# Transformer block on one core: ScalarE scales two of three norms of the second stage, and its order of work changes

## The chip, the cores and the metric

The kernel runs on one core of a Trainium2 chip. The metric is the time of one execution in device microseconds, from the first to the last instruction with what the runtime adds around it. Less is better.

## What is computed

For X of 16 batches x 512 tokens x 256 features, in float32, four parts follow one another; `ln` is a layer norm without gain or bias.

```python
x = x + A(ln(x))      # 16 heads of 64, softmax, exact gelu, product with Wpost, plus its own input
x = x + F(ln(x))      # W1, W2 rounded to -1, 0, 1; relu between; 256 -> 1024 -> 256
x = x + B(ln(x))      # 16 heads of 16 with rotary positions and biases
x = x + F(ln(x))      # the same feed-forward part again
```

`ln` is (x - mean) / sqrt(var + 1e-5) over the 256 features of a token.

## The kernel before, in words

Everything is laid out by hand: SBUF is one arena in which tiles have fixed places, and some share one. Each of the five engines gets its own list of instructions, written by a loop over the same schedule; semaphores tie them together. The first stage is part A, in slots from -21 to 541 (LAST_A); the second stage is the rest of the block. The second stage counts in steps, two to a slot: step = 2 * (slot - SHIFT) with SHIFT = 554. A batch s has its steps at 64 * s + r, where r is the number in the tables of lines 296 to 305. Since the tables reach from r = -115 to 152, up to four batches are in work at a time: while the attention scores of batch s are made (r = 0 to 62), the feed-forward part in front of batch s + 1 or s + 2 and the one behind batch s - 1 or s - 2 fill the gaps. The two kinds are called ffn0 (before attention B) and ffn1 (after it); the norm in front of attention B is "attn".

Matrix products are split for precision: a value is held as a high part (rounded, type float32r) and a low part (the rest). A product's result lands in one of three PSUM banks taken in turn (`fill % 3`, line 229); a fill waits until the one three before it has been emptied.

The places that the change and the prediction touch:

- Norm, VectorE (lines 1070 to 1093): `statistics` of two token blocks in each of two pieces, `aggregate` (mean and variance of four blocks, then variance + eps into `rstd`), and `normalise` in two pieces of two blocks, each block one `tensor_scalar` (x - mean) * rstd into `xn`. The pieces 0 to 4 stand at the five steps of NORM. GpSimd raises `rstd` to the power -0.5 (lines 529 to 531), one step after piece 2. It adds the output bias to x after xn is made (`add_bias`, line 533, at BIAS).
- TensorE transposes `xn` (XT0, XTB, XT1; line 735); ScalarE copies the result to `xh` (line 852), VectorE makes `xl` (line 1164). The up products (UP0, UP1) start when both transposes' banks are emptied. ScalarE applies Relu (line 860) and makes the high part `h_hi` (line 880, `hidden_high`), GpSimd the low part `h_lo` (line 543); the down products (DOWN0, DOWN1) wait for the low parts in turn.
- Attention B: TensorE makes scores at every even step (line 691), VectorE takes row maxima (line 1114), which travel through a transposition (line 761) and a DMA on SP's queue into two rows of `q_stack`; L = 11 slots later TensorE makes the transposed scores (line 705), ScalarE takes their exponential (line 838) and TensorE the product with the values (line 718), four key blocks to a quad of heads. The sum of a quad is copied from PSUM by ScalarE (`copy_values`, line 847, at r = 40, 56, 72, 88), and the next quad's first product waits for it. VectorE turns it (`invert_sums`, at INVERT) and scales it (`scale_heads`).
- Rotary part: ScalarE empties the query and key products with their bias (line 865), GpSimd rotates (lines 552 and 556, at ROTATE; the keys of batch 0 are VectorE's), ScalarE writes high parts (`parts_high`, line 898, at HIGHS), VectorE low parts (`parts_low`, line 1110, at LOWS), and SP stacks both by DMA into `q_stack` and `k_stack` (at STACK). `h_hi` and `h_lo` lie over the buffers of the rotation, so the first `hidden_high` of a batch waits for `roped`.
- SP: `load_ahead` loads x of a batch into `x_ahead` at r = -115, after the batch before has been stored back; `save_ahead` stores it at r = -54, once the attention bias is added.

ScalarE's order within a step is: empty the banks of the step before, high parts of the hidden tiles, high parts of queries or keys, copy of value sums, exponential:

## Time and profile before

| what | value |
|---|---|
| median of 3 runs | 3816.96 us (3816.83 to 3820.02) |
| profiled execution | 3815.57 us |
| its span | 3813.7 us |
| granted TensorE clock, mean | 0.982 |
| busy: TensorE, VectorE, ScalarE, GpSimd | 96%, 71%, 61%, 50% |
| second stage: first scores to last | 2274.5 to 3732.8 us |

The span is the time from the first to the last instruction of the one execution that was profiled; its own time is 1.9 us longer. TensorE's busy share is that of matmuls as the profile models them.

### The profile page before, as it was taken

Reading aid. Unit: us, or ns where it says so; the run is one execution under the profiler, and the core shown is the slowest. Engines: PE = TensorE matmul, PEld = TensorE weight load, DVE = VectorE, ACT = ScalarE, POOL = GpSimd, SP = SyncE. Lnnn points to the kernel's source line nnn. Section 1 sums busy time; section 2 is a strip of 40 time slices with the busy share of each in tenths; the row PEclk is TensorE's granted clock in tenths of the full one; section 3 lists DMA queues with packets and bytes.
Section 4 is the critical chain, followed back from the end, with each engine's and each line's share of the span. In section 5 each row is a group of like instructions: output and inputs, shape, how many; then the busy total and the mean of one; then the engine's idle time right before and its main releaser. Section 6 shows DMA issues by size and latency. Waiting matters only on the chain.

```text
span 3813.7 us, 64079 instructions
## 1 busy us (share of the span) xinstructions
PE 3650.5 (96%) x23938; PEld 2451.6 (64%) x23938; DVE 2720.9 (71%) x4342; ACT 2330.4 (61%) x4501; POOL 1917.1 (50%) x1210
## 2 busy tenths in 40 slices
PE   8999999999999999999999878999999999999987
PEld 5777777777777777777777654555555555555534
DVE  6766666667676666666667667888888888888762
ACT  5665666566566656656656435666666666666654
POOL 4555555545555555555555433555555555555412
PEclk9999999999999999999999988999999999999988
DMA  2000000000000000000000012222222222222220
GB/s 78 7 12 1 12 12 12 1 12 12 1 12 12 7 7 12 12 1 12 12 1 15 25 48 56 52 58 61 59 57 61 58 57 57 57 57 57 51 45 17
DMA packets 86965, 114.16 MB, mean 30 GB/s; under 512 B 6660, under 2 KB 60420, under 8 KB 86660
## 3 DMA queue, kind: packets, MB, share of 16 engines
q1 hardware_dynamic: 86660, 110.07, 11.5%
q8 instruction: 195, 3.19, 0.4%
q14 instruction: 110, 0.90, 0.1%
HBM read 33.43 MB, written 25.17 MB: 15 GB/s over the span
## 4 chain that ended last, share of the span: by engine, by line
PE 84%; DVE 9%; ACT 3%; issue 2%; POOL 2%; DMA 0%; DVEq 0%; POOLq 0%; ACTq 0%
PE ps_o L642 12%; PE ps_s L611 10%; PE ps_t L624 8%; PE ps_t L218 7%; PE ps_o L718 6%; PE ps_t L753 5%; PE ps_s L691 5%; PE ps_m L624 4%; PE ps_t L225 4%; PE ps_t L744 4%; PE ps_m L218 4%; PE ps_t L677 3%; DVE max_b L1114 3%; PE ps_s L705 3%; PE ps_m L744 2%
## 5 line engine op out<-in xcount | busy, mean ns | idle before, releaser
L511 POOL TENSOR_TENSOR e_a<-e_a,recip 128x1024 f32<-128x1024 f32 x512 | 969.4, 1894 | 955.7 <-DVE recip L983 955.6
L796 ACT ACTIVATE e_a<-ps_s,neg_max 128x512 f32<-128x512 f32 x1024 | 694.3, 685 | 548.5 <-DVE neg_max L976 548.2
L1114 DVE TENSOR_REDUCE max_b<-ps_s 128x2 f32<-128x1024 f32 x512 | 623.6, 1219 | 177.7 <-PE ps_s L691 176.0
L838 ACT ACTIVATE et<-ps_s 128x1024 f32<-128x1024 f32 x512 | 523.7, 1023 | 357.1 <-PE ps_s L705 356.8
L976 DVE TENSOR_REDUCE neg_max<-ps_s 128x2 f32<-128x1024 f32 x512 | 622.7, 1216 | 68.7 <-PE ps_s L611 68.7
L642 PE MATMUL ps_o<-et_a,v_a 128*64 128x256 f32 x4096 | 500.2, 386 | 9.6 <-DVE heads_a L1019 5.2
L611 PE MATMUL ps_s<-raw_a 64*128 64x512 f32 x3072 | 426.0, 409 | 8.8 <-ACT e_a L796 8.7
L543 POOL TENSOR_TENSOR h_lo<-h,h_hi 128x512 fp32r<-128x512 f32 x248 | 320.5, 1305 | 183.1 <-ACT h_hi L880 183.1
L642 PEld LDWEIGHTS ps_o<-et_a,v_a 128*64 128x64 f32 x4096 | 279.6, 137 | 192.8 <-issue 79.2
L990 DVE COPY et_a<-ps_t 128x512 f32<-128x512 f32 x366 | 250.9, 687 | 207.0 <-PE ps_t L624 202.8
L624 PE MATMUL ps_t<-ident,e_a 128*128 128x128 f32 x2660 | 395.0, 281 | 2.1 <-DVE xl L1164 2.0
L624 PEld LDWEIGHTS ps_t<-ident,e_a 128*128 128x128 f32 x2660 | 290.9, 141 | 133.4 <-issue 129.5
L531 POOL TENSOR_TENSOR rstd<-rstd,minus_half 128x4 f32<-128x4 f32 x48 | 49.0, 1021 | 642.6 <-DVE rstd L1085 642.6
L611 PEld LDWEIGHTS ps_s<-raw_a 64*128 64x128 f32 x3072 | 270.3, 185 | 132.5 <-issue 75.0
L691 PE MATMUL ps_s<-k_stack,q_stack 48*128 48x512 f32 x1024 | 264.0, 512 | 51.2 <-DVE max_b L1114 49.7
L718 PE MATMUL ps_o<-et,v_b 128*32 128x512 f32 x2048 | 281.5, 622 | 0.0
L803 ACT ACTIVATE et_a<-ps_t 128x512 f32<-128x512 f32 x299 | 178.3, 596 | 117.8 <-PE ps_t L624 117.7
L705 PE MATMUL ps_s<-q_stack,k_stack 50*128 50x512 f32 x1024 | 214.5, 412 | 30.4 <-ACT et L838 30.3
L691 PEld LDWEIGHTS ps_s<-k_stack,q_stack 48*128 48x128 f32 x1024 | 98.8, 189 | 215.2 <-DVE max_b L1114 100.6
L624 PE MATMUL ps_m<-ident,e_a 128*128 128x128 f32 x1436 | 224.7, 279 | 0.0
L1001 DVE SCALAR_TENSOR_TENSOR raw_a<-ps_t,raw_a 128x512 fp32r<-128x512 f32 x181 | 124.3, 686 | 129.3 <-ACT raw_a L822 124.4
L796 ACT ACTIVATION_READ_ACCUMULATOR e_a<-ps_s,neg_max 128x1 f32 x1024 | 202.9, 198 | 0.0
(196 smaller groups left out, 7315.7 us busy)
## 6 DMA issues: line engine op xcount, KB each, us to landing
q_stack<-roped_q SPq DMA_DIRECT2D x256, 96.0 KB
k_stack<-roped_k SPq DMA_DIRECT2D x256, 96.0 KB
x_a<-X SPq DMA_DIRECT2D x16, 512.0 KB, 3.9
X<-x_a SPq DMA_DIRECT2D x16, 512.0 KB, 2.9
x_ahead<-X SPq DMA_DIRECT2D x16, 512.0 KB, 3.8
X<-x_ahead SPq DMA_DIRECT2D x16, 512.0 KB, 4.9
x_before<-X SPq DMA_DIRECT2D x16, 512.0 KB, 3.8
OUT<-x_before SPq DMA_DIRECT2D x16, 512.0 KB, 5.1
```

The costliest lines, as they stand in the source:

```text
L218: last = nc.tensor.matmul(out, w[:, k, c0:c0 + P], xs[:, k, :], start=(i == 0), stop=(i == len(todo) - 1))
L511: nc.gpsimd.tensor_tensor(e_a[:, u % 5, :, :], e_a[:, u % 5, :, :], factor, ALU.mult).then_inc(e_normed, 1)
L611: last = mm(ps_s[:, 2 * j + h, :], raw[rows, q_part, c:c + P], raw[rows, k_part, :], start=(m == 0), stop=(m == 2))
L624: last = nc.tensor.transpose(bank(fill)[:, c:c + P], e_a[:, u % 5, j, t * P:(t + 1) * P], ident[:, :])
L642: last = mm(out, v_a[:, t, c:c + HA], et_a[:, 2 * (q % 2):2 * (q % 2) + 2, t, h, :], start=(t == 0), stop=(t == TB - 1))
L691: last = mm(ps_s[:, score_bank(u) + h, :], q_stack[rows, pair, block_ * P:(block_ + 1) * P], k_stack[rows, pair, :], start=True, stop=True)
L705: last = mm(ps_s[:, 2 + h, :], k_stack[rows, pair, keys * P:(keys + 1) * P], q_stack[rows, pair, :], start=True, stop=True)
L718: last = mm(ps_o[32 * h:32 * (h + 1), :], v_b[:, s % 2, keys, 4 * quad + h, :], et[:, (2 * w + h // 2) % 5, h % 2, :], start=(keys == 0), ...
L796: ins = nc.scalar.activation(e_a[:, u % 5, h, :], ps_s[:, 2 * (u % 2) + h, :], ACT.Exp, bias=neg_max[:, u % 5, h:h + 1], accum_out=sums[:, ...
L838: nc.scalar.activation(et[:, v % 5, :, :], ps_s[:, 2:4, :], ACT.Exp)\
L976: nc.vector.reduce_max(neg_max[:, u % 5, :], ps_s[:, 2 * (u % 2):2 * (u % 2) + 2, :], AX.X, negate=True)\
L1114: nc.vector.reduce_max(max_b[:, u // 4 % 2, :, u % 4], ps_s[:, score_bank(u):score_bank(u) + 2, :], AX.X, negate=True).then_inc(max_done, 1)
```

## The change

ScalarE now makes `xn` for the norms ffn0 and attn, as x * rstd + shift, with shift = -mean * rstd. VectorE writes -mean, GpSimd multiplies it with rstd behind the power. ffn1 stays on VectorE. In ScalarE's loop the exponential of a step comes before the high parts and the copy. The tables move: transposes of ffn0 two steps later, norm pieces of ffn0 and the last two of attn later, both biases later, high and low parts of queries and keys later, the first two stacks and INVERT one step or two, load and save of x_ahead.

```diff
+        shift = at("shift", 1.4375, [P, TB])
+        minus_mean = at("minus_mean", 1.46875, [P, TB])
...
-        XT0, UP0 = (-89.8, -88.8), (-83.9, -83, -81.5, -80, -79, -77.5, -76, -75)
+        XT0, UP0 = (-87.9, -86.9), (-83.9, -83, -81.5, -80, -79, -77.5, -76, -75)
...
-        NORM = {"ffn0": (-108, -106, -105, -103, -98), "attn": (-67, -64, -63, -60, -58), "ffn1": (103, 108, 109, 113, 115)}
-        BIAS = {"ffn0": -88, "attn": -57, "ffn1": 124}
-        ROTATE, HIGHS, LOWS = (-39, -37, -35, -34, -32, -30), (-34, -33, -29, -28), (-31, -30, -28, -26)
-        STACK = (-18, -16, -11, -9, 5, 7, 21, 23)
-        INVERT, SCALE_HEADS = (42, 58, 74, 90), (46, 62, 76, 92)
+        NORM = {"ffn0": (-101, -100, -98, -91, -89), "attn": (-67, -64, -63, -51, -49), "ffn1": (103, 108, 109, 113, 115)}
+        BIAS = {"ffn0": -86, "attn": -45, "ffn1": 124}
+        ROTATE, HIGHS, LOWS = (-39, -37, -35, -34, -32, -30), (-31, -29, -23, -21), (-28, -26, -20, -18)
+        STACK = (-17, -15, -11, -9, 5, 7, 21, 23)
+        INVERT, SCALE_HEADS = (43, 59, 75, 91), (46, 62, 76, 92)
...
+        nth_shift = {(part, s): n for n, (_, part, s) in enumerate(norm for norm in norms if norm[1] != "ffn1")}
...
-                            if r == -115:
+                            if r == -108:
                                 load_ahead(s)
-                            if r == -54:
+                            if r == -44:
                                 save_ahead(s)
...
                 def inverse_deviation(part, s):
                     pool.wait_ge(var_ready, nth_norm[part, s] + 1)
                     nc.gpsimd.tensor_tensor(rstd[:, :], rstd[:, :], minus_half[:, :], ALU.pow).then_inc(rstd_ready, 1)
+                    if part != "ffn1":
+                        pool.wait_ge(rstd_ready, nth_norm[part, s] + 1)
+                        nc.gpsimd.tensor_tensor(shift[:, :], minus_mean[:, :], rstd[:, :], ALU.mult).then_inc(shift_ready, 1)
...
+                def normalise(part, s, first):
+                    act.wait_ge(shift_ready, nth_shift[part, s] + 1)
+                    if part == "ffn0" and s == 0:
+                        act.wait_ge(a_x_out, 16 * (BATCH - 1))
+                    for t in (first, first + 1):
+                        nc.scalar.activation(xn[:, t, :], x_of[part][:, t, :], ACT.Identity, scale=rstd[:, t:t + 1],
+                                             bias=shift[:, t:t + 1]).then_inc(xn_ready, 1)
...
                         for todo in steps_of.get(step - 1, []):
                             empty(*todo)
+                        if step % 2 == 0 and 0 <= step // 2 - L < UNITS_ALL:
+                            exps(step // 2 - L)
                         for kind, part, i, s, fill in steps_of.get(step - 2, []):
...
                                 copy_values(QUADS * s + (r - 40) // 16)
-                        if step % 2 == 0 and 0 <= step // 2 - L < UNITS_ALL:
-                            exps(step // 2 - L)
+                        for piece, part, s in norm_steps.get(step, []):
+                            if piece > 2 and part != "ffn1":
+                                normalise(part, s, 2 * (piece - 3))
...
                     link(ins)
+                    nc.vector.tensor_scalar(minus_mean[:, :], mean_var[:, :, 0], -1.0, None, ALU.mult)
                     nc.vector.tensor_scalar(rstd[:, :], mean_var[:, :, 1], EPS, None, ALU.add).then_inc(var_ready, 1)
...
-                            else:
+                            elif part == "ffn1":
                                 normalise(part, s, 2 * (piece - 3))
```

## Rows read from the trace of the kernel before

**Rows 1.** The page, part 1: busy us, share of span, instructions.

```profile
PE 3650.5 (96%) x23938; PEld 2451.6 (64%) x23938; DVE 2720.9 (71%) x4342; ACT 2330.4 (61%) x4501; POOL 1917.1 (50%) x1210
```

**Rows 2.** Busy by stretch: batches 0, 1, 6; stretch: its us, then each engine's busy us.

```profile
2274.48:2353.55 79.07, 65.92 (x355) 36.13 (x355) 60.83 (x84) 42.04 (x59) 33.14 (x24) 0.85 0.21 48
2353.55:2441.14 87.59, 78.67 (x449) 41.26 (x449) 71.57 (x109) 54.48 (x74) 37.03 (x26) 0.92 0.25 56
...
2815.75:2909.41 93.66, 90.15 (x547) 52.46 (x546) 76.32 (x111) 62.75 (x90) 47.13 (x34) 1.00 0.25 58
```

**Rows 3.** Waits, us in total, times, longest: first of batches 0 and 1, then of period 6.

```profile
PE ps_s L691 <- DVE max_b L1114: 20.5, 23, 2.8
...
ACT et L838 <- PE ps_s L705: 21.1, 13, 2.8
```

**Rows 4.** Timeline of TensorE in period 6, with idle time before: start us, us.

```profile
2830.13 0.49 PE L705 MATMUL ps_s<-q_stack,k_stack 50*128 50x512 f32 x2 [0.84 <-ACT et L838]
...
2835.55 0.39 PE L753 MATMUL ps_m<-w,h_hi 128*128 128x256 f32 x1 [0.27 <-POOL h_lo L543]
...
2871.45 0.50 PE L705 MATMUL ps_s<-q_stack,k_stack 50*128 50x512 f32 x2 [1.25 <-ACT et L838]
...
2876.94 0.50 PE L691 MATMUL ps_s<-k_stack,q_stack 48*128 48x512 f32 x2 [0.86 <-DVE max_b L1114]
```

**Rows 5.** Timeline of ScalarE around steps 8 to 12 and 36 of that period.

```profile
2826.95 0.69 ACT L860 ACTIVATE h<-ps_t,b 128x512 f32<-128x512 f32 x1 [0.27 <-PE ps_t L744]
2827.53 1.14 ACT L880 ACTIVATE h_hi<-h 128x512 fp32r<-128x512 f32 x2
2828.58 0.58 ACT L847 ACTIVATE weighted<-ps_o 128x512 f32<-128x512 f32 x1
2829.05 1.02 ACT L838 ACTIVATE et<-ps_s 128x1024 f32<-128x1024 f32 x1
2829.96 0.69 ACT L860 ACTIVATE h<-ps_m,b 128x512 f32<-128x512 f32 x1
...
2832.78 0.69 ACT L860 ACTIVATE h<-ps_t,b 128x512 f32<-128x512 f32 x1 [0.56 <-PE ps_t L744]
2833.50 0.63 ACT L880 ACTIVATE h_hi<-h 128x512 fp32r<-128x512 f32 x1
...
2870.30 1.00 ACT L838 ACTIVATE et<-ps_s 128x1024 f32<-128x1024 f32 x1
```

**Rows 6.** Timeline of GpSimd at the same two places.

```profile
2834.21 1.28 POOL L543 TENSOR_TENSOR h_lo<-h,h_hi 128x512 fp32r<-128x512 f32 x1 [0.44 <-ACT h_hi L880]
...
2869.27 2.35 POOL L537 TENSOR_TENSOR x_ahead<-x_ahead,b_rows 128x1024 f32<-128x1024 f32 x1
```

**Rows 7.** Groups by line, batches 2 to 14: count, busy us, mean ns of one.

```profile
L1092 DVE TENSOR_SCALAR xn<-x_ahead,mean_var,rstd 128x256 f32<-128x256 f32 x100 | 96.3, 1002 | 0.0
...
L531 POOL TENSOR_TENSOR rstd<-rstd,minus_half 128x4 f32<-128x4 f32 x38 | 38.7, 1018 | 502.8 <-DVE rstd L1085 502.8
...
L865 ACT ACTIVATE q_flat<-ps_m,bqk 128x512 f32<-128x512 f32 x13 | 9.0, 690 | 2.1 <-PE ps_m L218 1.9
```

**Rows 8.** Timeline of VectorE in period 6: two low parts of keys.

```profile
2869.55 2.62 DVE L1110 TENSOR_TENSOR roped_k<-k_rot,roped_k 128x512 fp32r<-128x512 f32 x1
...
2873.82 0.68 DVE L1110 TENSOR_TENSOR roped_k<-k_rot,roped_k 128x512 fp32r<-128x512 f32 x1
```

**Rows 9.** The page, part 6: DMA issues, KB each, us to landing.

```profile
x_ahead<-X SPq DMA_DIRECT2D x16, 512.0 KB, 3.8
X<-x_ahead SPq DMA_DIRECT2D x16, 512.0 KB, 4.9
```

**Rows 10.** Timeline of TensorE ahead of the first scores, with idle time before.

```profile
2236.38 0.39 PE L225 MATMUL ps_t<-wb_hi,xh 128*128 128x256 f32 x1 [1.02 <-DVE x_a L1013]
...
2241.96 0.38 PE L677 MATMUL ps_t<-wpost_hi,heads_parts 128*128 128x256 f32 x1 [2.45 <-DVE x_a L1013]
...
2253.42 0.77 PE L744 MATMUL ps_t<-xh,w 128*128 128x512 f32 x1 [3.95 <-DVE xl L1164]
```

More of the change, by code:

```diff
@@ L166, in hybrid_block_kernel @@
         a_xn_ready = sem("a_xn_ready")
+        shift_ready = sem("shift_ready")
         xn_ready = sem("xn_ready")
@@ L1088, in normalise @@
                     dve.wait_ge(rstd_ready, nth_norm[part, s] + 1)
-                    if part == "ffn0" and s == 0:
-                        dve.wait_ge(a_x_out, 16 * (BATCH - 1))
                     for t in (first, first + 1):
```

## Prediction

> **What bounds the kernel now.** I read the page first: TensorE is busy 96% of the span [rows 1]. A change on ScalarE, VectorE and GpSimd can therefore give back only the time in which TensorE waits for them. Then the stretches of the second stage [rows 2]. Its batches repeat: from the scores of batch 6 at 2815.75 us to those of batch 7 at 2909.41 a period takes 93.66 us, and TensorE is busy for 90.15 of them. Only 3.5 us a period can be won, over twelve such periods (batches 2 to 13) about 42 us. The first two batches are looser: 79.07 - 65.92 = 13.2 us and 87.59 - 78.67 = 8.9 us without a matmul, most of it VectorE's (20.5 us in two periods end with a row maximum) [rows 3].
>
> Below, "step k" is a place in a period: scores(u) stands at every even step, 32 to a period. I follow the stalls of one period in the timeline of TensorE [rows 4]: 0.84 us at step 10 and 1.25 us at step 38, both for an exponential of ScalarE; 0.27 us at step 12 for a low part of GpSimd; 0.86 us at step 42 for a maximum. With crumbs under 0.2 us that is the 3.5 us.
>
> **Part by part, in one steady period.**
>
> *Exponential in front, step 10.* ScalarE does a Relu (2826.95), two high parts (2827.53), the copy of the value sums (2828.58) and then the exponential (2829.05), which ends at about 2830.0 [rows 5]; TensorE resumes at 2830.13 [rows 4]. Of the two high parts one belongs to step 7 and stays ahead. The exponential now starts after it, at 2828.1, and ends at 2829.05, when its reader would naturally come: the 0.84 us go. But high part and copy now follow: 0.57 + 0.47 us (the distances of starts in [rows 5]), so the copy ends at 2830.1. The next values product waits for that copy (it overwrites what is copied) and would be ready at 2830.13 - 0.84 + 0.24 = 2829.5. The new wait is 0.6 to 0.7 us where 0.84 went; I take a gain of 0.4 with the rounding of starts.
>
> *The same at step 12.* Here it costs. The last high part starts at 2833.50, its low part at 2834.21, and TensorE's down product waits for that until 2835.55 [rows 4, 5, 6]. Now the exponential of step 12, started when the Relu of 2832.78 is done, stands between them: 0.91 us later (2829.05 to 2829.96, the next start), less the 0.4 just won: the last low part, and with it TensorE, is 0.5 us later than before. Over steps 0 to 14 the period thus loses 0.5 us: the gain of step 10 is inside a stall that grew. The bias add moved away from this place (2.4 us of GpSimd among the low parts) does not help, since GpSimd is idle 0.44 us before the last low part.
>
> *Norms to ScalarE, eight activations a period.* They take off VectorE eight operations of 1002 ns mean [rows 7], 8.0 us a period. Their price on ScalarE no row shows. Bounds: above, a 128x512 Identity with a bias, 0.69 us; below, half of a 128x512 copy of 0.58 us, 0.29 us [rows 5, 7]. I take 0.41 us by starts. Two in a step are 0.8 us, at steps 13, 15, 37, 39. The cover is that ScalarE idles around the down product: it waits for scores 21.1 us in a period, up to 2.8 us at a time [rows 3]. If that cover were gone, 3.3 us a period would show. The rows have activations with one operand read per partition: 0.69 against 0.58 us for a copy [rows 5, 7]. By the Trainium skill ("ScalarE: Activation LUTs", What ACT_TABLE_LOAD costs) each such operand adds about 93 ns, and these have two; that would be 0.49 us each and 0.3 us more wait at step 40, 3 us in all.
>
> *The shift on GpSimd,* one multiply of 128x4 behind each power. The power on the same 128x4 is 1.02 us [rows 7], the nearest row and the upper bound; below, nothing. I take 0.5, the middle, since neither end is nearer. For the attention norm it is free (GpSimd then waits). For the feed-forward norm power and shift now stand between the rotations of the keys, so rotated keys come 1.2 us later. VectorE's extra multiply of 128x4 is 0.1 us, three times a period, before the variance goes out.
>
> *Rounded queries and keys later, steps 36 to 46.* Before, ScalarE waits for rotated keys and its exponential starts late at 2870.30 [rows 5]; this 1.25 us stall goes, since the keys' high parts move to steps 41 and 43. VectorE's low part of a key that took 2.62 us (a plain one is 0.68) fell on the bias add of GpSimd at 2869.27 [rows 6, 8]; its lateness made the 0.86 us of step 42. So 2.2 us (with crumbs) are removed. What is late next: VectorE still owes, from step 36 to 48, six maxima (1.15 us by starts), four low parts, two halves of xl, two adds, four statistics, a transposition with reciprocal: about 15.5 us, for a natural 15.1 us of TensorE. Also the transposes moved from step 38 to 40, so the second xl now comes after the add that waits for the last wo product; the up product of step 44 waits about 0.65 us for it. At step 40 the transposes wait 0.15 us for ScalarE's last scale of step 39, and the maximum there, whose PSUM bank the first xl frees, makes it 0.5 us in all. The maxima of steps 44 and 46: 0.3 us each. Sum of new waits 1.8, net gain 0.4 us.
>
> *High part of the first hidden tile.* It overwrites the buffers of the rotation and waits for the last key low part, now at the same step 46 on VectorE instead of eight steps earlier. ScalarE stands there some 2.4 us with an exponential and Relus behind it. Its slack before step 50 is about 1.5 us less the work it catches up: I take 0.3 us on TensorE; bounds 0 and 0.9 us.
>
> *SP's queue.* Save and load of x_ahead move to step 20, behind the two DMAs of one pair's maxima and ahead of two stacks (eight DMAs), the save of x_before and the maxima of the next pair. Landing takes 4.9 and 3.8 us [rows 9]; the statistics that need it stand seven steps later, 10 us. The stacks go out 5 us later, and their readers are 28 steps off. Cost 0; if the cover is gone, up to 1 us a period.
>
> A period: 0.5 - 0.4 + 0.3 = +0.4 us, twelve times +5.
>
> **Before the stage and in its first two batches.** Between 2221 and 2254 us TensorE waits 1.02 and 2.45 us for residual adds of VectorE and 3.95 us for xl [rows 10]. VectorE was in xn operations of batch 1 (5 us, stretched under GpSimd's rotations) and key rotations. With xn on ScalarE, and its copies no longer behind key high parts, I take 5.5 of these 7.4 us. In batches 0 and 1, sixteen xn operations leave a VectorE that is the bound at steps 2 to 18 and 34 to 42; two thirds of their excess shows less the later lows: 5.5 us. Together -11.
>
> **Sum:** +5 - 11 = -6 us. The profiled execution took 3815.57 us (span 3813.7, 1.9 around it), 1.4 below the median of three, 3816.96. Forecast 3811 on the median's scale, rounded to 3810.
>
> **Rivals.**
> - *Relief carries over (faster).* If VectorE, 8 us lighter, comes early into steps 36 to 48, the 1.8 us of new waits there shrink by 1.2: a period is -0.8, twelve are -10, and with -11 it is 3796. For: VectorE had no pause before step 36, and now has. Against: the lows and xl stand in the same steps now.
> - *GpSimd and VectorE collide at step 38 to 40 (slower).* The feed-forward bias add starts when ScalarE's last scale of step 39 is done; by my times 0.4 to 0.7 us after VectorE should begin its second query low part. It decides from the point where VectorE is later than that, which a shift of over about 0.85 us brings. Then that low part takes 2.6 us instead of 0.68, as the key's did [rows 8], the maximum of step 40 is late by 2 us, and a period loses 2.0 more: 3810 + 24 = 3834. The Trainium skill ("SBUF — State Buffer", SBUF: two separate sides) has it that the two share a port pair as an exclusive lock held for the whole instruction; by that rule, the row of 2.62 us agrees.
> - *ScalarE is the late one (slower).* Upper bound of the wait of step 46, 0.9, and the last low part of the feed-forward also 0.3 late: +1.2 a period, +14 in place of +5, and if the longer chain (shift, then ScalarE) also takes 5 of the start's 11: 3816.96 + 14 - 6 = 3825. It decides where the last low part of VectorE ends over 1.5 us after ScalarE is ready for it.
> - *Nothing moves:* TensorE-bound, each stall replaced by an equal one, 3817.
>
> **Chances.** A measurement of this kernel can tell about 0.2%, 7.6 us. Forecast (3803 to 3816) 0.37, half of it beyond 7.6 us; relief 0.28; collision 0.18; ScalarE late 0.11; nothing 0.06. Faster: 0.18 + 0.27 = 0.45; slower 0.18 + 0.07 = 0.25; same 0.30. The range reaches from below the relief case to the collision: 3789 to 3834.
>
> **What would show it.** Stalls of a period: at step 10 for "weighted" instead of "et", about 0.65 us; at step 12 for h_lo above 1 us; none at 38; at 44 for xl 0.65. The scales on ScalarE at 0.5 us of duration; the bias add not inside a query low part. Score starts of batch 0 at about 2269 instead of 2274.5. I am wrong if a period is below 93 or above 95 us, or if the start brings nothing.

## The result, and the profile after

The changed kernel takes 3838.12 us (median of 5, 3836.44 to 3841.64) where the kernel before takes 3816.96 (median of 5, 3810.02 to 3820.02): ratio 1.0059, 95% interval 1.0048 to 1.0070. It is 0.6% slower; 3810 was forecast, and 3838.12 lies above the range. The profiled execution has a span of 3837.5 us, 23.8 more than before.

The page of the changed kernel, part 1 (busy us, share of the span, instructions), beside [rows 1]:

```profile
PE 3647.6 (95%) x23938; PEld 2446.4 (64%) x23938; DVE 2573.1 (67%) x4262; ACT 2388.2 (62%) x4629; POOL 1907.4 (50%) x1242
```

VectorE lost 148 us of work and ScalarE gained 58, yet the kernel is longer: TensorE, busy as long as before, waits more. (A wait here is time in which an engine stands idle before an instruction.) The same stretches as in [rows 2], batches 0, 1 and 6, by their score starts (us, then busy us of each engine, granted clock, DMA):

```profile
2264.09:2342.14 78.05, 66.41 (x356) 36.28 (x355) 54.63 (x78) 45.49 (x67) 32.39 (x26) 0.85 0.22 51
2342.14:2429.35 87.21, 76.57 (x450) 40.14 (x449) 65.10 (x104) 57.84 (x82) 35.95 (x28) 0.96 0.25 56
2813.87:2910.01 96.14, 90.33 (x546) 52.45 (x546) 66.48 (x106) 66.34 (x98) 46.23 (x36) 1.00 0.24 56
```

| stretch | before | after | difference |
|---|---|---|---|
| to the first scores of batch 0 | 2274.5 | 2264.1 | -10.4 |
| batches 0 and 1 | 166.7 | 165.3 | -1.4 |
| batches 2 to 13, mean of a period | 93.73 | 96.13 | +2.40, twelve times +28.8 |
| batch 14 | 86.3 | 90.1 | +3.8 |
| from the first scores of batch 15 | 161.5 | 164.5 | +3.0 |

The last two rows are not alike. In batch 14 TensorE is busy 80.15 us at a mean granted clock of 0.89, where it was 77.42 us at 0.92: 2.7 of the 3.8 us are busy time, at a lower clock. From batch 15 on it is busy 129.7 us at 0.86 in both kernels, so the 3.0 us are waits.

The periods of the changed kernel all lie between 96.11 and 96.15 us. TensorE's timeline in period 6, all matmuls with idle time of over 0.1 us ahead (compare [rows 4]; `x8` counts the instructions merged into a line, the bracket has the wait before it and what ended it):

```profile
2828.34 1.07 PE L725 MATMUL ps_o<-et,v_b 128*32 128x512 f32 x8 [0.60 <-ACT weighted L862]
2834.19 0.39 PE L760 MATMUL ps_m<-w,h_hi 128*128 128x256 f32 x1 [1.13 <-POOL h_lo L550]
2840.44 0.50 PE L698 MATMUL ps_s<-k_stack,q_stack 48*128 48x512 f32 x2 [0.19 <-DVE max_b L1131]
2870.75 0.50 PE L698 MATMUL ps_s<-k_stack,q_stack 48*128 48x512 f32 x2 [0.69 <-DVE max_b L1131]
2874.31 0.27 PE L768 MATMUL ps_t<-ident,max_b 128*8 128x128 f32 x1 [0.93 <-DVE xl L1181]
...
2878.85 0.70 PE L751 MATMUL ps_m<-xh,w 128*128 128x512 f32 x2 [0.87 <-DVE xl L1181]
2881.11 0.50 PE L698 MATMUL ps_s<-k_stack,q_stack 48*128 48x512 f32 x2 [0.17 <-DVE max_b L1131]
2884.14 0.50 PE L698 MATMUL ps_s<-k_stack,q_stack 48*128 48x512 f32 x2 [0.15 <-DVE max_b L1131]
2887.72 0.51 PE L712 MATMUL ps_s<-q_stack,k_stack 50*128 50x512 f32 x2 [0.24 <-ACT et L845]
2898.64 0.39 PE L760 MATMUL ps_t<-w,h_hi 128*128 128x256 f32 x1 [0.38 <-POOL h_lo L550]
2906.23 0.51 PE L698 MATMUL ps_s<-k_stack,q_stack 48*128 48x512 f32 x2 [0.43 <-DVE max_b L1131]
```

They stand at steps 10, 12, 18, 40, 40, 44, 46, 48, 50, 56 and 62. Gone are the 0.84 us at step 10 and the 1.25 and 0.86 of steps 38 and 42; in all TensorE waits 5.8 us where it waited 3.5. Three places are looked at first, and the experiments took them apart.

*Step 12.* ScalarE's timeline ahead of the 1.13 us:

```profile
2827.60 0.60 ACT L862 ACTIVATE weighted<-ps_o 128x512 f32<-128x512 f32 x1
2828.08 0.70 ACT L875 ACTIVATE h<-ps_m,b 128x512 f32<-128x512 f32 x1
...
2830.57 0.69 ACT L875 ACTIVATE h<-ps_t,b 128x512 f32<-128x512 f32 x1 [0.24 <-PE ps_t L751]
2831.24 1.03 ACT L845 ACTIVATE et<-ps_s 128x1024 f32<-128x1024 f32 x1
2832.17 0.62 ACT L895 ACTIVATE h_hi<-h 128x512 fp32r<-128x512 f32 x1
```

The last Relu is done at 2831.26, and its high part starts 0.9 us later, behind the exponential; the low part and the down product follow it.

*Steps 43 to 46.* VectorE's timeline there:

```profile
2877.41 0.69 DVE L1148 TENSOR_TENSOR x_before<-x_before,ps_m 128x512 f32<-128x512 f32 x1 [1.14 <-PE ps_m L741]
2878.02 0.68 DVE L1181 TENSOR_TENSOR xl<-ps_t,xh 128x512 fp32r<-128x512 f32 x1
2878.62 0.27 DVE L1184 TENSOR_TENSOR m_rows<-ps_t,m_rows 8x128 fp32r<-8x128 f32 x1
2878.82 0.69 DVE L1161 STREAM_TRANSPOSE token_rows<-weighted 128x512 f32<-128x512 f32 x1
2879.54 0.25 DVE L1163 RECIPROCAL recip_b<-token_rows 128x16 f32<-128x16 f32 x1
2879.83 1.23 DVE L1131 TENSOR_REDUCE max_b<-ps_s 128x2 f32<-128x1024 f32 x1
...
2884.25 0.68 DVE L1127 TENSOR_TENSOR roped_k<-k_rot,roped_k 128x512 fp32r<-128x512 f32 x1
```

The turning of the weighted sums and their reciprocal (1.0 us by starts, from 2878.82 to 2879.83) now come behind xl. VectorE waits 1.14 us just before the residual add, in a gap which they used to fill (before, the add at 2879.87 waited 0.26); behind them stand the maximum of step 44, for which the scores of step 46 wait, and both low parts of the keys, and for the second of these ScalarE waits:

```profile
2885.02 0.63 ACT L895 ACTIVATE h_hi<-h 128x512 fp32r<-128x512 f32 x1 [2.11 <-DVE roped_k L1127]
```

*Steps 40 to 44.* The transposes of the feed-forward norm went two steps later, the up product did not: 0.93 us for the bank that the first xl frees, 0.87 for the second xl. The 0.69 us ahead of them, for a maximum, are taken up under two_fixes_stats.

### The profile page after: what moved, and what is told of

Its sections match the earlier page's. It is cut to its first block, busy times and chain, and to the rows that moved or that the text cites. A ratio compares the mean times of both kernels' runs of the same rounds, so it can differ in the third digit from the quotient of the medians.

```text
span 3837.5 us, 64188 instructions
## 1 busy us (share of the span) xinstructions
PE 3647.6 (95%) x23938; PEld 2446.4 (64%) x23938; DVE 2573.1 (67%) x4262; ACT 2388.2 (62%) x4629; POOL 1907.4 (50%) x1242
## 4 chain that ended last, share of the span: by engine, by line
PE 75%; DVE 11%; ACT 7%; issue 5%; POOL 2%; DMA 0%; DVEq 0%; ACTq 0%; POOLq 0%
PE ps_o L649 12%; PE ps_s L618 10%; PE ps_t L631 8%; PE ps_t L221 8%; PE ps_o L725 5%; PE ps_t L228 4%; PE ps_m L631 4%; PE ps_m L221 4%; PE ps_t L760 4%; DVE max_b L1131 4%; PE ps_s L698 4%; PE ps_t L684 3%; POOL h_lo L550 2%; ACT et L845 2%; PE ps_s L712 2%
## 5 line engine op out<-in xcount | busy, mean ns | idle before, releaser
L760 PE MATMUL ps_t<-w,h_hi 128*128 128x256 f32 x752 | 197.6, 299 | 10.2 <-POOL h_lo L550 9.8
```

## The experiments

Times are medians in us, each with the ratio to the kernel before on the same chip (3814.54 us beside the first four, 3815.88 beside the next, 3815.61 beside the last); "first scores" is the start of batch 0's scores, "period" the mean of the twelve, both from the profiled execution.

| kernel | time | ratio (95%) | first scores | period |
|---|---|---|---|---|
| norms_only | 3846.56 | 1.0080 (1.0065 to 1.0096) | 2273.3 | 96.58 |
| exp_front_only | 3837.8 | 1.0060 (1.0043 to 1.0077) | 2275.3 | 95.66 |
| tables_only | 3885.38 | 1.0182 (1.0167 to 1.0197) | 2269.1 | 99.09 |
| after_old_order | 3874.25 | 1.0151 (1.0136 to 1.0166) | 2264.4 | 98.67 |
| invert_back | 3814.1 | 0.9996 (0.9987 to 1.0006) | 2264.6 | 94.60 |
| transposes_back | 3851.5 | 1.0093 (1.0078 to 1.0109) | 2263.9 | 96.45 |
| last_high_first | 3825.74 | 1.0026 (1.0015 to 1.0037) | 2264.8 | 95.29 |
| all_three | 3815.69 | 0.9999 (0.9990 to 1.0009) | 2264.6 | 94.51 |
| two_fixes | 3803.05 | 0.9970 (0.9958 to 0.9981) | 2264.3 | 93.78 |
| two_fixes_stats | 3796.8 | 0.9956 (0.9941 to 0.9971) | 2263.4 | 93.56 |
| two_fixes_xl | 3793.35 | 0.9945 (0.9930 to 0.9959) | 2264.6 | 93.18 |
| two_fixes_both | 3786.22 | 0.9928 (0.9913 to 0.9943) | 2265.6 | 92.70 |

### The three parts of the change, one at a time

**norms_only**: the scales on ScalarE at the old steps, everything else as before (the lines shown are against the kernel before).

```diff
+                        for piece, part, s in norm_steps.get(step, []):
+                            if piece > 2 and part != "ffn1":
+                                normalise(part, s, 2 * (piece - 3))
```

> The change's norms alone: ScalarE scales ffn0 and attn, GpSimd makes the shift, but every table and the order of ScalarE's work are those of before. My theory (the longer period comes from the new places and the new order, not from the move of the scaling): the start of the scores comes some 5 us earlier, a steady period is 93.65 us plus or minus 0.7, since VectorE's 0.86 us of step 42 shrinks and two scales at steps 4 and 6 push ScalarE's exponentials of step 8 back; total 3808 to 3822 us. Rival (scales on ScalarE and the shift between the rotations are the cost): a period of 95 us or more and a total over 3830 us.

Measured: 32 us slower, not equal; the rival's figures came. The first scores come 1.2 us earlier, not 5, and the 0.86 us of step 42 stays. At steps 4 and 6 the scales of the attention norm fall among the Relus and high parts of ffn1; ScalarE's timeline in period 4 (steps 4 to 6) has no gap there:

```profile
2640.78 1.02 ACT L845 ACTIVATE et<-ps_s 128x1024 f32<-128x1024 f32 x1
2641.69 1.08 ACT L853 ACTIVATE xn<-x_ahead,shift,rstd 128x256 f32<-128x256 f32 x2
...
2645.24 1.10 ACT L853 ACTIVATE xn<-x_ahead,shift,rstd 128x256 f32<-128x256 f32 x2
```

The exponentials of steps 8 and 10 are late by 0.45 and 1.72 us where only 0.84 was. So the later places of the scales are no ornament: at the old ones the scales on ScalarE cost time. The waits come to 1.3 us more than before, and the shortest periods to 95.23 us, 1.6 more; the rest of the 96.58 is the clock (below).

**exp_front_only**: the kernel before with the exponential in front.

```diff
                             empty(*todo)
+                        if step % 2 == 0 and 0 <= step // 2 - L < UNITS_ALL:
+                            exps(step // 2 - L)
                         for kind, part, i, s, fill in steps_of.get(step - 2, []):
...
                                 copy_values(QUADS * s + (r - 40) // 16)
-                        if step % 2 == 0 and 0 <= step // 2 - L < UNITS_ALL:
-                            exps(step // 2 - L)
```

> The kernel before with one edit: the exponential in front of high parts and copy. My theory: step 10 waits 0.6 us for the copied sums in place of 0.84 for the exponential, step 12 about 1.1 us for the low part in place of 0.27, step 56 about 0.4 us for the low part; the 1.25 us of step 38 goes but comes back as about 1.1 us for a row maximum at step 40, because VectorE is behind there. A period of 94.4 to 94.8 us, the start as before (2274 us), total 3826 to 3832 us. Rival (the exponential in front is what gains, the tables lose): a period under 93 us, total under 3808 us.

Measured 95.66, beyond both figures. The down product waits 0.96 us at step 12, as the chain says. At step 38 the 1.25 us for the exponential are gone, but the scores of step 40 now wait 1.62 us (0.09 before) for a maximum that stands behind the long key low part (2.63 us under GpSimd's bias add, as in [rows 8]): one lateness had covered the other. Step 10 waits 0.70 us for a row maximum (ended 2837.69), not for the copied sums: ahead of that maximum VectorE's scales took 2.58 and 1.70 us a pair, beside low parts of GpSimd. New is 1.25 us for a maximum at step 54. VectorE's timeline, then GpSimd's:

```profile
2899.40 2.95 DVE L1092 TENSOR_SCALAR xn<-x_before,mean_var,rstd 128x256 f32<-128x256 f32 x2
2902.28 1.21 DVE L1114 TENSOR_REDUCE max_b<-ps_s 128x2 f32<-128x1024 f32 x1
```

```profile
2899.41 4.18 POOL L543 TENSOR_TENSOR h_lo<-h,h_hi 128x512 fp32r<-128x512 f32 x3 [1.42 <-ACT h_hi L880]
```

The same two operations take 1.01 us at this place in the kernel before, where they start at 2890.55 and share only half a microsecond with a low part (2889.79 to 2891.08). Here two low parts, at 2899.41 and 2900.90, start with them: with the exponentials in front, GpSimd's low parts fall onto them. The Trainium skill ("SBUF — State Buffer", SBUF: two separate sides) has the two engines hold their shared port pair as an exclusive lock; the rows of 2.63 and 2.95 us agree.

**tables_only**: the kernel before with all new places, VectorE's norms and the old order.

```diff
-        INVERT, SCALE_HEADS = (42, 58, 74, 90), (46, 62, 76, 92)
+        INVERT, SCALE_HEADS = (43, 59, 75, 91), (46, 62, 76, 92)
...
-        XT0, UP0 = (-89.8, -88.8), (-83.9, -83, -81.5, -80, -79, -77.5, -76, -75)
+        XT0, UP0 = (-87.9, -86.9), (-83.9, -83, -81.5, -80, -79, -77.5, -76, -75)
```

(with NORM, BIAS, HIGHS, LOWS, STACK, load and save as in the change)

> The kernel before with all new places (transposes of ffn0, norm pieces, biases, high and low parts, stacks, INVERT, load and save), but norms on VectorE and the old order on ScalarE. My theory: the places alone lose most: about 0.9 us at step 42 and 0.9 at step 44 for xl, 0.4 at step 62 for a maximum behind INVERT, the exponential of step 46 now stands behind the wait for the last low part, and scales at steps 37 and 39 add 2 us on VectorE where it is late anyway: a period of 97 to 100 us, total 3855 to 3895 us. Rival (places are harmless by themselves): a period below 94.5 us.

**after_old_order**: the changed kernel with the exponential last in its step.

```diff
-                        if step % 2 == 0 and 0 <= step // 2 - L < UNITS_ALL:
-                            exps(step // 2 - L)
                         for kind, part, i, s, fill in steps_of.get(step - 2, []):
...
                                 copy_values(QUADS * s + (r - 40) // 16)
+                        if step % 2 == 0 and 0 <= step // 2 - L < UNITS_ALL:
+                            exps(step // 2 - L)
```

> The changed kernel with ScalarE's old order (exponential last, the scales behind it). My theory: the 1.13 and 0.38 us for low parts at steps 12 and 56 and the 0.60 for the copied sums go, 0.84 for the exponential of step 10 returns, and the exponential of step 46 stands behind the wait for the last key low part, 1.5 to 2.5 us: a period of 95.8 to 97.5 us against 96.13, total 3832 to 3856 us. Rival (the new order is the whole loss): a period of 94.2 us or less, total under 3815 us.

tables_only came inside its range (99.0 us in nearly all its periods), after_old_order above its own. With the new tables the exponential in front is worth 36 us (3874.25 against 3838.12, and 98.67 against 96.13 a period); with the old ones it costs 23. Why, ScalarE's timeline of after_old_order at step 46 shows:

```profile
2893.91 0.63 ACT L895 ACTIVATE h_hi<-h 128x512 fp32r<-128x512 f32 x1 [3.36 <-DVE roped_k L1127]
2894.45 1.00 ACT L845 ACTIVATE et<-ps_s 128x1024 f32<-128x1024 f32 x1
```

The exponential is queued behind the high part that waits for the last key low, and TensorE waits 1.97 us for it. In front, the exponential is out before that wait. But the waits alone are not the 36 us: they sum to 6.1 us a period against 5.8. TensorE's busy time is 92.84 us against 90.33, at half clock behind the wait of 1.97 us (last section). Between tables_only and after_old_order lies the norm's engine alone: it is worth 11 us, 4.7 of them before the first scores, 3.5 in batches 0 and 1 and 4.6 in periods 2 and 3; the later periods are nearly equal, 99.0 to 99.1 us against 99.0, and what follows batch 14 is 3.3 us longer with ScalarE's.

### Which places cost the 2.4 us of a period

**invert_back**: the changed kernel, reciprocals back.

```diff
-        INVERT, SCALE_HEADS = (43, 59, 75, 91), (46, 62, 76, 92)
+        INVERT, SCALE_HEADS = (42, 58, 74, 90), (46, 62, 76, 92)
```

> The changed kernel with one table entry as before: the reciprocals of the sums at steps 42, 58, 10, 26 of a period instead of 43, 59, 11, 27. If the wait of 0.43 us for a maximum at step 62 comes from the reciprocal of step 59, which stands behind the residual add there, it goes and nothing comes: a period is 95.6 to 95.8 us instead of 96.13, the kernel about 5 us shorter than the changed one, 3831 to 3835. Rival: the reciprocal of step 42 stood ahead of the maximum which waited 0.86 us in the kernel before, and makes that wait again: a period of 96.1 to 96.9, 3837 to 3847.

Measured 94.60 us a period, 1.53 less, three times what I expected of it, and 3.6 us less in batch 14, though not by its waits: TensorE is busy 76.04 us there at a clock of 0.94, against 80.15 at 0.89. VectorE's timeline at the same place:

```profile
2870.82 1.23 DVE L1131 TENSOR_REDUCE max_b<-ps_s 128x2 f32<-128x1024 f32 x1 [0.80 <-PE ps_s L698]
2871.97 0.70 DVE L1161 STREAM_TRANSPOSE token_rows<-weighted 128x512 f32<-128x512 f32 x1
2872.70 0.25 DVE L1163 RECIPROCAL recip_b<-token_rows 128x16 f32<-128x16 f32 x1
2873.21 0.69 DVE L1148 TENSOR_TENSOR x_before<-x_before,ps_m 128x512 f32<-128x512 f32 x1 [0.26 <-PE ps_m L741]
...
2874.62 1.20 DVE L1131 TENSOR_REDUCE max_b<-ps_s 128x2 f32<-128x1024 f32 x1
```

Turning and reciprocal fill the gap ahead of the residual add; the maximum of step 44 follows xl at once. The waits of steps 46, 48, 50 and 62 are gone (0.17 + 0.15 + 0.24 + 0.43 = 0.99 us), that of step 56 is 0.31. The other 0.5 us of the 1.53 show in TensorE's busy time (89.84 us in place of 90.33 a period by the records), and they stand beside the same waits. From the scores of one step to those of the next, step 44 is shorter by 0.24 us, 46 by 0.22, 50 by 0.50, 56 by 0.06 and 60 by 0.50, in all 1.52. Step 50, for instance, takes 3.30 us with 0.24 us of wait in the changed kernel and 2.80 without one here. So what a wait costs is better read from start to start than from the idle time, since the ends of matmuls are modelled.

**last_high_first**: at step 12 the high part of the last hidden tile goes ahead of the exponential.

```diff
+                        behind = any(kind == "up" and i == 7 for kind, part, i, s, fill in steps_of.get(step - 2, []))
-                        if step % 2 == 0 and 0 <= step // 2 - L < UNITS_ALL:
+                        if not behind and step % 2 == 0 and 0 <= step // 2 - L < UNITS_ALL:
                             exps(step // 2 - L)
...
                                 hidden_high(part, i, s, fill)
+                        if behind and step % 2 == 0 and 0 <= step // 2 - L < UNITS_ALL:
+                            exps(step // 2 - L)
```

> The changed kernel, but at a step where the high part of the last hidden tile is due the exponential stands behind that high part (step 12 alone). The down product of step 12 waits 1.13 us for the last low part where it waited 0.27 before. My theory: that is the exponential of the same step standing ahead, so the wait falls to 0.2 to 0.5 us and the exponential, 0.57 us later, has that much slack: a period is 95.2 to 95.5 us, the kernel 3826 to 3832. Rival: the delay is inherited from ScalarE's later steps 8 to 11, or the exponential becomes late in its place: a period of 95.9 to 96.3, 3834 to 3840.

As expected: the wait is 0.27 us again, as in [rows 4], and a period 95.29. The exponential took no harm.

**transposes_back**

```diff
-        XT0, UP0 = (-87.9, -86.9), (-83.9, ...
+        XT0, UP0 = (-89.8, -88.8), (-83.9, ...
-        NORM = {"ffn0": (-101, -100, -98, -91, -89), ...
+        NORM = {"ffn0": (-101, -100, -98, -93, -91), ...
-        BIAS = {"ffn0": -86, ...
+        BIAS = {"ffn0": -88, ...
```

> The changed kernel with the transposes of the feed-forward norm at step 38 again instead of 40, its scales at steps 35 and 37 instead of 37 and 39, its bias add at 40. My theory: the waits at step 40 (0.93 us for a PSUM bank that the first xl frees, part of the 0.69 us for a maximum) and at step 44 (0.87 us for xl) come of the two steps by which the transposes went later while the up product stayed. Then they go but for some tenths, and a period is 94.2 to 95.2 us, the kernel 3814 to 3827. Rival: VectorE has too much to do from step 36 to 48 whatever the order; xl earlier only makes the maxima of steps 38 to 42 later by as much: a period of 95.8 to 96.8, 3833 to 3845.

The rival held for the period: 95.87 us in the shortest, 96.45 in the mean. The bank wait of step 40 stays (0.89), the 0.87 of step 44 and the 0.69 of step 40 go, the scores of step 42 wait 0.86 for a maximum, and those of step 46 wait 0.51 where it was 0.17. The two steps alone were not to blame. The total lies above even the rival's, by the clock: in batches 0 and 1, 6.9 us longer than in the changed kernel, TensorE is busy 149.97 us at 0.86 in place of 142.98 at 0.91, and four of the twelve periods have a stretch at half clock.

**all_three**: the three edits together.

> The changed kernel with all three edits: reciprocals, transposes, the high part of the last hidden tile. If the three act at different steps, the gains add: 0.4 + 1.4 + 0.8 = 2.6 us a period, 93.5 us, with the start of the changed kernel (scores of batch 0 at 2264 us) 3802 to 3812, faster than both. If they share one slack (VectorE's from step 36 to 62), the sum is less than the parts: 94.3 to 95.5 a period, 3815 to 3830.

The total fell within the rival's range, 3815 to 3830. Four of its twelve periods last 93.5 us, the sum I had worked out; the others about 95. Two neighbouring periods (5 and 6), in which TensorE waits at the same steps for as long (within 0.01 us each), show the difference:

```profile
2718.17:2813.16 94.99, 91.76 (x546) 53.03 (x546) 68.60 (x106) 66.37 (x98) 46.31 (x36) 0.98 0.24 57
2813.16:2906.68 93.52, 90.24 (x545) 52.42 (x544) 68.65 (x106) 66.37 (x98) 46.31 (x36) 1.00 0.25 58
```

TensorE is busy 1.5 us longer at a clock of 0.98: it is the clock, not a wait. Batches 0 and 1 are 4.9 us longer than in the changed kernel, with less waiting (18.3 us in place of 22.3) and more busy time at a lower clock (151.82 us at 0.84 in place of 142.98 at 0.91). So the three edits add in their waits, and the clock takes the gain back.

### Towards a better version

**two_fixes**: invert_back and last_high_first together, transposes as in the change.

> The changed kernel with the reciprocals back and the last hidden tile's high part ahead of the exponential. Measured apart, the one took 1.53 us off a period (96.13 to 94.60), the other 0.84 (to 95.29). They act at other steps (42 to 62, and 12), so they should add: 93.76 us a period, 12 x 2.37 = 28 us below the changed kernel, 3802 to 3809, faster than before by the start it gained (10 us). Rival: the two share ScalarE's backlog of steps 46 to 56, and the period stays at 94.4 or above, 3811 or more.

93.78, forecast 93.76: the two add, and the kernel is 0.3% faster than before (interval 0.19 to 0.42%). Its periods are those of the kernel before (93.73) again; the gain is the earlier start.

**two_fixes_stats**: the statistics of ffn1 out of the way of the maximum of step 40.

```diff
-        NORM = {... "ffn1": (103, 108, 109, 113, 115)}
+        NORM = {... "ffn1": (109, 111, 112, 115, 117)}
```

> As the run before it, with the statistics of the second feed-forward norm at steps 45 and 47 instead of 39 and 44, its mean at 48 instead of 45, its scales at 51 and 53. Theory that VectorE's order decides the 0.69 us wait for a maximum at step 40 (a rounding and 0.75 us of statistics stand ahead of that maximum): the wait goes to 0 to 0.1 and the next ones stay: 93.0 to 93.3 us a period, 5 to 9 us less than the run before it. Rival: the wait for the PSUM bank at step 40 (0.93) takes it over, since it hangs on ScalarE's high part of x behind its exponential: it grows to 1.4 to 1.6 and the period changes by less than 0.2.

Neither: the waits of step 40 stay at 0.69 and 0.93 as if nothing had been moved. TensorE's and VectorE's timelines:

```profile
2857.35 0.50 PE L698 MATMUL ps_s<-k_stack,q_stack 48*128 48x512 f32 x2 [0.69 <-DVE max_b L1134]
```

```profile
2854.79 0.68 DVE L1130 TENSOR_TENSOR roped_q<-q_rot,roped_q 128x512 fp32r<-128x512 f32 x1
2855.39 0.68 DVE L1151 TENSOR_TENSOR x_before<-x_before,ps_t 128x512 f32<-128x512 f32 x1
2855.99 1.22 DVE L1134 TENSOR_REDUCE max_b<-ps_s 128x2 f32<-128x1024 f32 x1
2857.12 0.68 DVE L1130 TENSOR_TENSOR roped_q<-q_rot,roped_q 128x512 fp32r<-128x512 f32 x1
```

The scores of step 40 start when the maximum that ends at 2857.21 has freed their bank: that of step 38. I had put the wait down to the maximum of its own step, but the statistics stood behind the one that counts; ahead of it are the first query low part and a residual add. The period falls by 0.22 all the same: from scores to scores, step 56 is shorter by 0.59 us (the 0.34 of wait for a low part are gone) and step 54 longer by 0.39 (0.21 of wait for xn). Batch 14 and what follows give 4.5 us.

**two_fixes_xl**: the second transposed half ahead of the wo product.

```diff
-        XT0, UP0 = (-87.9, -86.9), (-83.9, ...
+        XT0, UP0 = (-87.9, -87.7), (-83.9, ...
```

> As the first run of the three, with the second transposed half of the first feed-forward norm before the wo product of step 40 instead of behind it, so that its low part comes at step 42 instead of 43. Theory that the 0.91 us wait of the first up product at step 44 is only that low part standing behind the residual add of the same step: it falls to 0 to 0.3, a period is 92.9 to 93.3, 5 to 10 us less. Rival: the low part, now ahead of the maximum of step 42 or the residual add, makes these late by as much (a wait of 0.5 to 0.9 for a maximum at step 42 or 44): the period changes by less than 0.3.

The 0.91 us at step 44 go whole (the step is 0.96 us shorter), but step 50 is longer, 3.11 us in place of 2.79, with 0.04 us of wait for an exponential: 93.18, 0.60 less. ScalarE stands 1.68 us at step 46 for the last key low part, ahead of that exponential.

**two_fixes_both**

> Both of these edits on the first run of the four. If each acts on a wait of its own: 92.3 to 92.7 us a period, 3785 to 3795. If steps 38 to 44 hold one backlog of VectorE: no better than the better of the two by over 0.3 us a period.

92.70 a period, 3786.22 us: 0.72% faster than before (0.57 to 0.87%), 52 us below the changed kernel. Together the two edits give more than their sum, 1.08 us against 0.22 + 0.60: with both, ScalarE stands 1.13 us for the last key low part, and step 50 takes 2.79 us again. TensorE's timeline, the idle times of over 0.15 us that remain in period 6:

```profile
2812.79 1.06 PE L725 MATMUL ps_o<-et,v_b 128*32 128x512 f32 x8 [0.59 <-ACT weighted L862]
...
2854.36 0.50 PE L698 MATMUL ps_s<-k_stack,q_stack 48*128 48x512 f32 x2 [0.69 <-DVE max_b L1134]
2857.92 0.27 PE L768 MATMUL ps_t<-ident,max_b 128*8 128x128 f32 x1 [0.93 <-DVE xl L1184]
```

(0.27 at step 12 and 0.20 at step 18 besides.)

## Why the prediction was wrong

The forecast was a sum of -11 before and in the first two batches and +0.4 us a period. The first held: -11.8. The second was +2.40, and that is the miss: 28.8 us of twelve periods where 5 were forecast. The sum had no term for batch 14 and the end, which took 6.8 us more. From scores to scores in period 6, against the kernel before:

| steps | forecast | changed kernel | with the reciprocals back |
|---|---|---|---|
| 0 to 14 | +0.5 | +0.51 | +0.51 |
| 14 to 36 | 0 | 0.0 | 0.0 |
| 36 to 48 | -0.4 | +0.34 | -0.15 |
| 48 to the next period | +0.3 | +1.63 | +0.57 |

- **The step that failed is "Rounded queries and keys later, steps 36 to 46".** It listed "a transposition with reciprocal" among the 15.5 us VectorE owes there and gave its new place no price: as a sum of work against a sum of time, the order inside could not show. There was room enough by that measure: VectorE is busy 14.5 of the 17.6 us from step 36 to 48 of the changed kernel (the list, by the distances of starts, adds up to 14.2 and not to 15.5). Moved from the gap ahead of the residual add to behind xl, it put 1.0 us in front of the maximum of step 44 (for which the scores of step 46 wait) and the key lows, and as much at step 59, which the prediction does not name. invert_back shows its price: 1.53 us of the 2.40, 0.5 of it in steps 36 to 48 and 1.06 behind them.
- **The same step's new waits**, forecast 1.8, measured 0.69 + 0.93 + 0.87 + 0.17 + 0.15 = 2.8, of which 0.3 are the reciprocal's. "makes it 0.5 us in all" was 0.69 and 0.93. The xl at step 44 was 0.87 for 0.65 forecast. What the part removed (1.25 and 0.86) went as said.
- **Exponential in front.** Step 10: forecast 0.6 to 0.7 for the copy, measured 0.60. Step 12: forecast above 1 us, measured 1.13. Steps 0 to 14 cost 0.51 us, forecast 0.5: this part was right in mechanism and size. last_high_first shows that the loss was avoidable: it takes 0.84 us off.
- **First high part, step 46.** ScalarE stands 2.11 us (forecast 2.4), TensorE waits 0.24 at step 50, which goes with the reciprocal, and 0.38 for a low part at step 56, which stays at 0.31. Forecast 0.3; step 56 alone is 0.6 us longer than before, and this term the sum did not have. That it is ScalarE's standing at step 46 that makes this low part late is likely and not shown.
- **Norms to ScalarE.** The scale takes 589 ns, two in a row 1.08 us: 0.49 by starts, not my 0.41. Groups by line of the changed kernel (x count | busy us, mean ns):

```profile
L853 ACT ACTIVATE xn<-x_ahead,shift,rstd 128x256 f32<-128x256 f32 x128 | 68.9, 589 | 8.8 <-POOL shift L538 8.8
...
L538 POOL TENSOR_TENSOR shift<-minus_mean,rstd 128x4 f32<-128x4 f32 x32 | 8.0, 249 | 2.5
```

  In the periods ScalarE never waits ahead of a scale (its 8.8 us are two waits at the start), and no matmul of period 6 waits for one. The price that the Trainium skill gives ("ScalarE: Activation LUTs", What ACT_TABLE_LOAD costs: 186 ns + 0.833 ns an element + 93 ns for each pointer operand) makes an estimate of 585 ns for 256 elements and two pointers; the row of 589 agrees.
- **Shift on GpSimd**: 0.25 us mean where I took 0.5. **SP's queue**: no wait came of it, as said.
- **Start and first batches**: -10.4 and -1.4 where I had -5.5 and -5.5. The total is right, the halves are not: that the sum held is in part luck. Between the transposes of 2221.04 us (now 2218.34) and the up product of 2253.42 us (now 2243.76), where the forecast looked for its 5.5, TensorE won 7.0 us; 2.7 more came ahead of them. In batches 0 and 1 the waits for a row maximum fell only from 20.5 to 18.4 us. tables_only brings 5.4 us before the first scores, norms_only 1.2, both together 10.1.
- **The end.** Of the 3.0 us from batch 15 on, all are waits, and no run here shows which part makes them.
- **The rivals.** None came true. The collision of bias add and query low did not come (the low part takes 0.68 us), and no run has a relief that carries over: VectorE has 9.8 us less to do in a period, and TensorE waits for it at more places. "ScalarE late" was right in where (steps 50 and 56) but foresaw +1.2 for another reason. "I am wrong if a period is above 95 us" is what came.

## What to carry to other kernels

When hand-placed work moves, price each item by what stands directly behind it in its engine's queue, not by the engine's total in the stretch: here 0.95 us of work that filled a gap of its engine, landed one step later behind the gap at four places of a period, cost 1.53 us a period, all of it behind two of them. A change of order is worth what it is worth with a given table: the same move of the exponential cost 23 us with the old places and gave 36 with the new, most of the 36 by the clock; so measure parts both alone and taken out of the whole, and make an exception at the one step where the order hurts.

## What was not expected of the hardware

TensorE's clock can turn a wait into more than itself. In norms_only, periods 4 and 6 have the same waits at steps 8 to 42 (0.45, 1.72, 0.29, 0.19, 1.25, 0.86), but one is 1.5 us longer. Stretches of four microseconds from some 0.4 us before the wait of 1.72 us at step 10 ends (at 2649.41 and 2843.24), in period 4 and in period 6 (us, busy of TensorE, weight loads, VectorE, ScalarE, GpSimd, clock, DMA):

```profile
2649.00:2653.00 4.00, 3.59 (x21) 1.68 (x22) 1.59 (x4) 3.40 (x7) 3.50 (x3) 1.00 0.50 150
...
2842.90:2846.90 4.00, 3.66 (x13) 1.52 (x14) 1.03 (x3) 2.44 (x5) 3.42 (x3) 0.58 0.46 147
```

Behind the same wait, 21 matmuls ran in one and 13 in the other, at a granted clock of 0.58, between the two levels of 2.4 GHz (1.00) and 1.2 GHz (0.50). In after_old_order it followed the 1.97 us wait of step 48 (TensorE busy 3.69 of the 6 us before, clock 0.93) in a full stretch at half clock:

```profile
2895.72:2901.72 6.00, 6.00 (x19) 3.37 (x23) 1.36 (x3) 4.61 (x9) 2.92 (x4) 0.50 0.44 87
```

It explains why its period is 98.98 us with 6.1 us of waits, where the changed kernel with 5.8 has 96.14: TensorE's busy time is 92.84 us against 90.33.

A long wait is not needed. all_three has no wait of over 0.91 us in a period, but those of 0.90 at step 40 and 0.86 at step 42 end 1.1 us apart. From the end of the second, in periods 5 and 6:

```profile
2778.30:2782.30 4.00, 4.00 (x16) 1.63 (x16) 2.64 (x4) 1.97 (x2) 0.00 (x0) 0.63 0.00 0
...
2873.29:2877.29 4.00, 4.00 (x23) 1.96 (x24) 3.71 (x7) 2.47 (x3) 0.00 (x0) 1.00 0.01 4
```

In the 4 us before, TensorE was busy 2.24 us in both. Where the clock fell in periods 2 to 13:

| kernel | waits at or just behind which it fell | periods |
|---|---|---|
| before | 1.25 at step 38 | 7, 10 |
| norms_only | 1.72 at step 10 | seven of twelve |
| norms_only | 1.25 at step 38 | 5, 9, 12 |
| exp_front_only | 1.62 at step 40 | 2 |
| tables_only | 1.34 and 0.51 at step 40 | 3 to 13 |
| tables_only | 1.98 at step 48 | 2 |
| after_old_order | 1.97 at step 48 | 3 to 13 |
| transposes_back | 0.89 and 0.86 at steps 40 and 42 | 4, 5, 6, 8 |
| all_three | 0.90 and 0.86 at steps 40 and 42 | eight of twelve |
| changed kernel and the other six | | none |

The changed kernel's waits of 0.69 and 0.93 us at step 40 end 3.6 us apart, and there it never fell; its twelve periods are equal within 0.04 us. So the kernels with one wait of 1.25 to 1.98 us, or with two shorter ones close together, lost busy time as well, from one period in twelve (exp_front_only) to eleven (after_old_order, some 2.5 us in ten of them). It also means that a time outside the steady periods says little about one edit: batches 0, 1, 14 and 15 run at granted clocks of 0.79 to 0.96 that differ from kernel to kernel.

What makes the clock fall after one such wait and not after its twin, these runs leave open.
